# The opening of the first batch in another order: keys and first maxima first, values later

## The reference

```python
xn  = groupnorm(x, 32 groups) * gn_w + gn_b
qkv = einsum('oc,bct->bot', qkv_w, xn) + qkv_b        # 1536 x 512
q, k, v = split per head (8 heads of 64 channels)
w   = softmax(q.T k * 64**-0.5)                       # 2304 x 2304 for each head
a   = einsum('bts,bcs->bct', w, v)
out = xn + proj_w @ a + proj_b
```

## Time and profile before

| | us |
|---|---|
| median of 3 runs | 3850.76 |
| lowest, highest | 3850.36, 3852.95 |
| the profiled execution's own time | 3851.22 |
| its span, first to last instruction | 3849.5 |
| PE busy in the span | 3737.8 (97%) |
| mean granted TensorE clock (1 is full) | 0.994 |

### The profile page before, as it was taken

One profiled execution on the slowest core, in us unless ns is written; L12 is line 12 of the kernel. 1 busy time (PEld: TensorE's weight loads), 2 busy tenths in 40 slices (PEclk: granted clock), 3 DMA queues, 4 the chain that ended last, 5 costly groups with the idle time before them and its releaser, 6 DMA issues.

```text
span 3849.5 us, 74532 instructions
## 1 busy us (share of the span) xinstructions
PE 3737.8 (97%) x30004; PEld 2293.1 (60%) x30004; DVE 2222.4 (58%) x2820; ACT 2875.1 (75%) x4037; POOL 2997.9 (78%) x1639
## 2 busy tenths in 40 slices
PE   6999999999999999999999999999999999999998
PEld 3565565655856556555675656555567565656556
DVE  4555556556555555655645565565655655555553
ACT  2777777787577777778757777777876777777784
POOL 0788888788388888878838888887874888888894
PEclk9999999999999999999999999999999999999999
DMA  2000012021400001202140000120123000000014
GB/s 79 14 23 24 17 35 63 25 58 37 143 20 19 23 22 31 71 16 59 43 137 19 23 22 17 37 67 21 55 70 109 22 19 23 20 20 19 20 36 136
DMA packets 133673, 165.02 MB, mean 43 GB/s; under 512 B 61648, under 2 KB 110800, under 8 KB 132816
## 3 DMA queue, kind: packets, MB, share of 16 engines
q1 hardware_dynamic: 133328, 160.26, 13.4%
HBM read 122.17 MB, written 38.04 MB: 42 GB/s over the span
## 4 chain that ended last, share of the span: by engine, by line
PE 88%; DVE 3%; POOL 2%; issue 2%; ACT 2%; DMA 1%; SPq 1%; POOLq 0%; ACTq 0%; DVEq 0%
PE oacc L604 26%; PE scores L583 22%; PE pool_bank L531 14%; PE aux_banks L553 12%; PE pool_bank L543 7%; PE scores L684 4%; POOL denom L1140 2%; PE pool_bank L570 1%; DVE o_norm L1003 1%; DVE maxima L905 1%; ACT probs L789 1%; DMA out<-probs 1%; PE scores L531 1%; ACT scores L802 1%; PE scores L543 0%
## 5 line engine op out<-in xcount | busy, mean ns | idle before, releaser
L1140 POOL TENSOR_TENSOR denom<-denom,probs 128x768 f32<-128x768 f32 x1536 | 2822.4, 1838 | 463.9 <-ACT probs L789 275.0
L905 DVE TENSOR_REDUCE maxima<-aux_banks 128x2 f32<-128x512 f32 x1728 | 1655.9, 958 | 1413.8 <-PE aux_banks L553 1382.4
L789 ACT ACTIVATE probs<-scores 128x768 f32<-128x768 f32 x1728 | 1309.0, 810 | 683.7 <-PE scores L583 678.5
L802 ACT ACTIVATE scores<-seeds 128x768 f32<-128x768 f32 x1728 | 1340.3, 821 | 13.5 <-PE scores L591 10.0
L604 PE MATMUL oacc<-probs,vals 128*64 128x384 f32 x6912 | 1276.8, 489 | 0.0
L604 PEld LDWEIGHTS oacc<-probs,vals 128*64 128x64 f32 x6912 | 498.7, 137 | 499.8 <-issue 309.4
L553 PE MATMUL aux_banks<-k_hi,q_hi 64*128 64x512 f32 (+1 forms) x3456 | 691.5, 396 | 43.2 <-DVE maxima L905 35.6
L553 PEld LDWEIGHTS aux_banks<-k_hi,q_hi 64*128 64x128 f32 x3456 | 322.9, 183 | 629.0 <-issue 462.2
L583 PE MATMUL scores<-q_hi,k_hi 64*128 64x384 f32 x3456 | 597.0, 341 | 11.3 <-ACT scores L802 10.9
L583 PE MATMUL scores<-q_lo,k_hi 64*128 64x384 f32 x3456 | 587.5, 335 | 0.0
L583 PE MATMUL scores<-q_hi,k_lo 64*128 64x384 f32 x3456 | 587.4, 336 | 0.0
(11 more groups left out here) (91 smaller groups left out, 1559.1 us busy)
## 6 DMA issues: line engine op xcount, KB each, us to landing
seeds<-neg_rows SPq DMA_DIRECT2D x96, 384.0 KB, 3.5
xtile<-x SPq DMA_DIRECT2D x72, 384.0 KB, 3.2
att<-o_norm SPq DMA_DIRECT2D x96, 192.0 KB, 1.9
probs<-x SPq DMA_DIRECT2D x24, 768.0 KB, 4.8
out<-probs SPq DMA_DIRECT2D x24, 768.0 KB, 6.7
xtile<-att SPq DMA_DIRECT2D x12, 768.0 KB, 5.0
att_raw<-att SPq DMA_DIRECT2D x12, 768.0 KB, 6.5
neg_rows<-neg_cols SPq DMA_DIRECT2D x384, 0.8 KB
```

The source lines that it names most:

```text
L789: a(prob(s).rearrange("p (h n) -> p h n", n=N), scores[:, s % 2, :, 0:N], ACT.Exp, scale=SCALE).then_inc(probs_ready, 1)
L802: a(scores[:, s % 2, :, 0:N], seeds[blk % 2][:, :].rearrange("p (e n) -> p e n", n=N), ACT.Copy).then_inc(seeded, 1)
L905: v.tensor_reduce(maxima[:, :, qt, kc], aux_banks[:, :, 0:UNIT_KEYS[kc % 2]], AX.X, ALU.max)\
L1140: gp.tensor_tensor(acc, acc, prob(s), ALU.add).then_inc(added, 1)
```

## The change

```diff
@@ first_order
-        order = [("groupmean", 0, 0), ("groupvar", 0, 0), ("bias", 0, 0), ("k", 0, 0), ("q", 0, 0)]
+        order = [("groupmean", 0, 0), ("groupvar", 0, 0), ("k", 0, 0), ("q", 0, 0)]
         for kc in range(CH):
             if kc + 1 < CH:
                 order.append(("k", 0, kc + 1))
-            order.append(("aux", 0, kc))
-            order.append(("v", 0, kc))
-            order += [("aux", qt, kc) for qt in range(1, QT)]
-        for c in range(1, EARLY_Q):
-            order.append(("q", 0, c))
-        return order + [("aux", u // CH, u % CH) for u in range(QT * CH, AHEAD)]
+            order += [("aux", qt, kc) for qt in range(QT)]
+        order += [("q", 0, c) for c in range(1, EARLY_Q)]
+        ahead = [("aux", u // CH, u % CH) for u in range(QT * CH, AHEAD)]
+        for g in range(VG):
+            order.append(("v", 0, g))
+            order += ahead[g * len(ahead) // VG:(g + 1) * len(ahead) // VG]
+            if g == VG // 2:
+                order.append(("bias", 0, 0))
+        return order
@@ SP, opening
             load_weights(wk, 1, D, wk_in)
+            send_max(0, 0)
             wait_full(sp, FIRST_USES["v", 0, VG - 1])
             load_weights(wv, 1, 2 * D, wv_in)
-            send_max(0, 0)
@@ ScalarE
             def batch(b, last):
-                a(warm[:, :], ones[:, 0:1], ACT.Exp)
                 stream(b, last)
                 projection(b, last)
 
             act.wait_ge(consts_made, 4)
+            a(warm[:, :], ones[:, 0:1], ACT.Exp)
             for s in range(2):
                 seed(s, 0, PRIMED)
@@ VectorE, opening
-            u = FIRST_USES["bias", 0, 0]
-            wait_full(dve, u)
-            v.tensor_tensor(pb, pb, bank(u)[:, 0:CT], ALU.add).then_inc(bank_free[u[0]], 1)
...
+                elif kind == "bias":
+                    wait_full(dve, u)
+                    v.tensor_tensor(pb, pb, bank(u)[:, 0:CT], ALU.add).then_inc(bank_free[u[0]], 1)
+                    dve.wait_ge(wproj_hi_ready, 1)
+                    v.tensor_tensor(wproj_lo[:, :, :], wproj_full, wproj_hi[:, :, :].bitcast(fp32),
+                                    ALU.subtract).then_inc(wproj_lo_ready, 1)
-            dve.wait_ge(wproj_hi_ready, 1)
-            v.tensor_tensor(wproj_lo[:, :, :], wproj_full, wproj_hi[:, :, :].bitcast(fp32),
-                            ALU.subtract).then_inc(wproj_lo_ready, 1)
```

## The result

| | before | after |
|---|---|---|
| median (lowest to highest), us, 7 runs each | 3850.76 (3850.17 to 3852.95) | 3862.96 (3861.94 to 3868.31) |
| span of the profiled execution | 3849.5 | 3861.8 |
| mean granted clock | 0.994 | 0.991 |

The ratio is 1.0032, 95% interval 1.002 to 1.0044: slower, and 3.0 above the forecast of 3860, inside its range. The forecast of 3860 lay 9.2 above the median before; the measured difference is 12.2. All times in this text are in us.

What follows compares the result with a forecast made beforehand. PE, busy 97% of the span, was taken to bound the kernel, with its waits and clock deciding. 3851.22 - 1.3 (-5.1 - 6.0 + 12.9 - 3.1) + 10.4 for clock falls gave 3860 us, range 3851 to 3865.

Steps and rivals of the forecast that it cites:

- Front: Before the first maxima unit: without the bias product, keys start at 27.2 and the first unit comes 5.1 us earlier.
- Loop and tail at full clock: First unit to second query preparation, -6.0 us; from there to banks opened, with values and bias product, +12.9.
- hand-over: Banks opened to second pair of probs-times-values done: 9.6 us instead of 12.74, -3.1, with bounds -3.5 and 0.
- The falls: Clock drops to half in the new loop's gaps and the bias product: 4.4 falls at 2.4 us each, +10.4.
- the two small gaps: Stretches of 3.5 us between two key preparations, PE working 1.0: a clock fall one in two each.
- the rival with half clock all through: Clock stays at half through the whole loop after the first fall: 3871 us, chance 0.05.
- The row at 744.7: Profile stretch before a clock fall about 748.1, PE busy 1.48 of 3.3 us: evidence that falls need no long stop.
- 88 to 92.7: Old tail's stretch of bare units, PE busy 1.27 us before the clock fell: the likeness for the new loop's gaps.
- from 110 us on every batch has the lengths of before: Sign for the rest of the kernel: instruction streams are the same after 110 us, so batch lengths do not change.
- That the clock holds: Rival: three units in 3.5 to 4.8 us and six in 8.5 suffice; no falls, 3849.9 us, chance 0.07.
- few falls: Rival: only the 8.5 us gap, perhaps the bias product, brings the clock down: 3852.3 to 3854.7 us, chance 0.18.

Runs made afterwards that it cites:

- fill_half_after: The changed kernel with extra unread matmuls, 0.68 to 1.7 us, in each of PE's waits of the key loop: 3853.87 us, ratio 1.0009 to the kernel before.
- warm_only: The kernel before with only the one-column exponential (table load) moved ahead of the first seeds: 3852.32 us, ratio 1.0002.
- low_behind: The changed kernel with VectorE's maximum of a round's first unit ahead of the low part of the newest keys: 3856.17 us, ratio 1.0018 to the kernel before.
- v_in_loop: The changed kernel with each value group back behind the first unit of its round: 3851.82 us, ratio 1.0003 to the kernel before.

## Why the prediction was right, point by point

- **Front, forecast -5.1:** -6.3. Keys start at 27.52 for 27.2; the clock rose during the first keys (4.14 for 5.39). In the experiments with the same instructions up to there the first unit came between 36.8 and 38.4, so -4.7 is as good an answer. The -6.3 lies 0.1 outside the bounds.
- **Loop and tail at full clock, -6.0 and +12.9; hand-over -3.1:** 36.17 - 41.97 = -5.8, 25.38 - 12.39 = +13.0, 9.74 - 12.74 = -3.0, from fill_half_after. The bias product took 3.73 for 3.5, and VectorE's and ScalarE's parts were hidden. At full clock the changed opening ends at 109.63 for 110.17, -0.5 where -1.3 was forecast; half of the difference is the front (-4.7 for -5.1), the rest 0.1 to 0.2 in each of the three other stages.
- **Of the hand-over** the gain is the clock's and wproj_lo's; warm_only shows none for the table load. The prediction had not split it.
- **The falls, 4.4 at 2.4:** seven, at 40.5, 47.3, 57.6, 67.8, 74.6, 101.9 and 112.2. I took the two small gaps for even chances and both fell, and did not count the hand-over, where the table load now keeps PE waiting for the seeds (112.24) and the clock fell too. The price of one fall was below the forecast: at 121.00 against 109.63 the seven cost 11.4, or 13.0 with the 1.6 by which this front was better, so 1.6 to 1.9 each. The count was too low and the price too high, and the product, 10.4 for 11 to 13, came near because the two errors cancel: that part is luck. (4.4 x 2.4 is 10.6, not 10.4; and the rival with half clock all through counts five keys where the loop has four, which makes it 2.6 too dear.)
- **The row at 744.7** carries less than the prediction puts on it: it is the start of a stop of PE of 6.17, and the clock fell 1.9 into that stop. Its busy 1.48 of 3.3 was not spread as in the new loop, where work and short waits alternate. The likeness that did hold was that with 88 to 92.7.

```profile
752.35 0.80 PE L553 MATMUL aux_banks<-k_hi,q_hi 64*128 64x512 f32 x2 [6.17 <-DVE maxima L905]
```

- **The later 1.8** at 1057 was not foreseen: "from 110 us on every batch has the lengths of before" holds only up to falls that a profile has or has not.
- **The rivals.** That the clock holds is refuted by the trace, that it stays at half throughout as well (full again at 44.0, 54.2, 61.0, 71.3 and 84.9), and few falls too. The section "HAM oscillation — how this bites in real kernels" of the Trainium skill's page "TensorE: Matmul & The Clock Gate" says that the return of the clock is paid at every tile, and the trace agrees: there was a fall in each of the loop's five stretches between two preparations. The idle gap to which it ties the fall did not occur: PE's longest stop in the loop was 2.04. The measurement decides: here the clock fell in stretches that short matmuls broke up. That the uncovered waits themselves are the price fell with fill_half_after, which kept them all and took back 8.4 of the 12.2.

## What to carry to other kernels

Order work on PE so that something dense stands in every wait for another engine, in pieces as long as the wait. What such a wait costs is not only itself but the halved clock of the dense work behind it, which the changed loop paid at all five of its gaps and low_behind, with shorter gaps, at two. A pair of work items that hide each other (values beside maxima) should not be separated into a stretch with waits and a stretch without. Before sizing a filler, count matmuls against records in the trace.

## What was not expected of the hardware

- The clock can fall with PE busy for much of the time: in the changed loop PE was busy for 27.03 of 44.48 us (61%) and the clock stood at 0.73 on average; before, at 34.75 of 41.97 (83%), it stayed at 1.00, but in the profile of warm_only, with the same loop, it fell once.
- When it rises is not fixed: with the same instructions from 27.5 on, the first keys took 4.14 in one profile and 5.39 in another, and the first unit moved by 1.6 us. Differences of 1 to 2 us between single profiles of these kernels mean nothing for that reason.
- One-column matmuls with their loads keep PE busy without a gap (98.18 to 101.9), and the clock is at half right behind them (0.51 from 101.90 on) in three of the five profiles that have them in one piece in the tail; in v_in_loop it was at half all through them.
